# Attention maxima interleaved with halves of the scores, and turned before they are combined

## The chip, the cores and the metric

The kernel runs on one core of a Trainium2 chip. The metric is device time in microseconds (us) of one execution; lower is better. The core has TensorE (PE in the rows, with its weight loads as PEld), VectorE (DVE), ScalarE (ACT), GpSimd (POOL) and SyncE (SP), each with an instruction queue of its own, worked off in order. They synchronise by semaphores.

## The reference

A small two-layer model runs on x of shape (4, 1024, 128): causal attention, an MLP, an RWKV-like time and channel mix, an MLP, a second causal attention, two mixtures of experts and a single-head attention. The change touches the two causal attentions of 16 heads alone. What they compute, per head:

```python
scores = einsum('bqhd,bkhd->bhqk', q, k)      # layer 0: head width 8, plus one shared rotary term of width 32
scores = where(causal, -inf, scores / scale)  # layer 1: latent of width 32
w = softmax(scores, axis=-1)
attn = einsum('bhqk,bkhd->bqhd', w, v)
```

## The kernel before, in words

`attention` (L619) serves both layers: layer 0 with G=4 heads in a group and 4 groups for a batch, layer 1 with G=2 and 8 groups. One step is one group of one batch, so layer 0 has 16 steps and layer 1 has 32. Queries and keys are held as bf16 pieces (hi, mid, lo), stacked along the contraction dimension.

The softmax is written so that the row maximum is subtracted inside the score matmul. It therefore has to be known before a step begins. The work for it runs ahead of the steps, in *maximum units*: one unit is one bf16 matmul of a block of 128 queries against at most 512 keys into a PSUM bank of `mx` (L801; there are two such banks, used in turn), and one VectorE reduction of that bank (L931 where no mask is needed, L935 with the causal mask, followed by the read of its accumulator). TensorE may write a bank of `mx` only when VectorE has read it (`s_mxf`). A group has 12G units: 8G *wide* ones (query blocks 7, 6, 5 and 4, two parts each) and 4G *narrow* ones (query blocks 3, 2, 1 and 0, of 512, 384, 256 and 128 keys).

A step goes through eight key blocks kb. For each head j, `scores` (L820) computes the transposed scores of 128 keys against all queries that see them: queries 0 to 511 are one half (for kb < 4 only), queries 512 to 1023 the other. Each half takes two matmuls (L833, L835) and, where it holds the diagonal, a 128-column mask matmul (L838). Both halves go to one of two double banks of `score`, and ScalarE takes the exponential of both in one instruction (L910), up to 1024 elements wide. After the scores of block kb come the f32 matmuls of `values` for block kb-1 (L855); after block 7 come those of blocks 6 and 7.

TensorE's order is written out by hand (L880 to L893). Behind the scores of each head in kb 0 to 3 stand two wide units of the next group; behind those of kb 5, 6 and 7 stand one, two and one narrow units of the group after next. VectorE goes through the same units in the same order. Behind the scores of kb 4, `turn_max` (L806) turns the finished maxima into rows. Before it, `finish_max` (L941) makes them out of the two parts with four small VectorE instructions, as bf16 hi and lo; after it, `copy_turned` (L954) copies the two turned pieces out of PSUM, which frees both banks of `mx`. SyncE sends the rows through DRAM into an extra row of the second query operand (L745, L747), which the next step waits for (L877). Behind the last narrow unit, VectorE copies the finished output out of PSUM (L993), sets the next values (L972), and only then begins the wide units of the next step.

Of the kernel before, what the change touches and what calls it, by code (L numbers as in the profile page):

```python
# [19 lines left out]
P = 128  # L20
# [598 lines left out]
def attention(nc, k, tag, cf, qp, kp, qs, ks, vsrc, o_scr, l_scr, m_scr):  # L619
# [15 lines left out]
    NPC = 8 * 4  # L635
    with ExitStack() as st:  # L636
# [8 lines left out]
        mneg = c.sb("mneg", [P, G * QT])  # L645
        mpc = c.sb("mpc", [P, 2, G * QT], BF16)
        mrow = c.sb("mrow", [G * QT, 2, P], BF16)
        osb = c.sb("osb", [P, 2, T])
        masked = c.sb("masked", [P, 2, CH], BF16)
        score = c.ps("score", [P, 2, 2, CH])  # L650
        outp = c.ps("outp", [P, 2, CH])
        mx = c.ps("mx", [P, 2, CH])
# [11 lines left out]
        s_dpassed = c.sem("vector_passed")  # L664
# [125 lines left out]
        def _(pe):  # L790
            def max_units(b, g, qts, j, u):

                n = b * GN + g
                R = cf.rows[0]
                for qt in qts:
                    for part in range(2 if qt >= 4 else 1):
                        lo, hi = part * CH, min((qt + 1) * P, (part + 1) * CH)
                        bank = mx[:, u % 2, :]

                        pe.wait_ge(s_mxf, n * MU + u + 1)  # L800
                        pe.matmul(bank[:, 0:hi - lo], Q0[0:R, g % 4, j, qt * P:(qt + 1) * P],  # L801
                                  K0[0:R, g % 4, j % KG, lo:hi], start=True, stop=True).then_inc(s_mx, 1)
                        u += 1
                return u

            def turn_max(b, g, u):  # L806
                n = b * GN + g

                pe.wait_ge(s_mc, 4 * n + 4)
                for p in range(2):  # L810
                    pe.wait_ge(s_mxf, n * MU + u + 1)
                    pe.transpose(mx[0:G * QT, u % 2, 0:P // 2].bitcast(BF16), mpc[:, p, :], k.identb[:]).then_inc(s_mx, 1)
                    u += 1
# [6 lines left out]
            def scores(b, g, kb, j):  # L820

                n = b * GN + g
                u = kb * G + j

                pe.wait_ge(s_exp, n * U + u + 1)
                for half in range(2):
                    lo, hi = max(half * CH, kb * P), (half + 1) * CH
                    if lo >= hi:
                        continue
                    diag = lo == kb * P  # L830
                    bank = score[:, u % 2, half, lo - half * CH:CH]
                    R0, R1 = cf.rows
                    pe.matmul(bank, K0[0:R0, g % 4, j % KG, kb * P:(kb + 1) * P], Q0[0:R0, g % 4, j, lo:hi],  # L833
                              start=True, stop=False)
                    last = pe.matmul(bank, K1[0:R1, g % 2, j % KG, kb * P:(kb + 1) * P], Q1[0:R1, g % 2, j, lo:hi],  # L835
                                     start=False, stop=not diag)
                    if diag:
                        last = pe.matmul(bank[:, 0:P], k.identb[:], k.maskkq[:], start=False, stop=True)  # L838
                last.then_inc(s_st, 1)

            def values(b, g, kb):
# [3 lines left out]
                pe.wait_ge(s_exp, n * U + (kb + 1) * G + 2)  # L845
# [14 lines left out]
            def all_max_units(b, g, parts, u):  # L860
                for qts in parts.values():
                    for j in range(G):
                        u = max_units(b, g, qts, j, u)
                return u

            await_rows0(0, 0)
            all_max_units(0, 0, WIDE, all_max_units(0, 0, NARROW, 0))
            turn_max(0, 0, NARROW_U + WIDE_U)
# [3 lines left out]
            def step(b, g):  # L872
# [6 lines left out]
                u1, u2 = NARROW_U, 0  # L879
                for kb in range(QT):  # L880
                    if kb == 5 and two:
                        await_rows0(*two)
                    for j in range(G):
                        scores(b, g, kb, j)
                        if kb in WIDE and one:
                            u1 = max_units(*one, WIDE[kb], j, u1)
                        if kb in NARROW and two:
                            u2 = max_units(*two, NARROW[kb], j, u2)
                    if kb == 4 and one:
                        turn_max(*one, u1)  # L890
                    if kb > 0:
                        values(b, g, kb - 1)
                values(b, g, QT - 1)  # L893

            over_batches(pe, step)

        @block.scalar
        def _(act):
            act.sem_inc(s_exp, 2)

            def step(b, g):
                n = b * GN + g
                for kb in range(QT):

                    act.wait_ge(s_pv, n * 8 + kb - 1 + NPC)
                    for j in range(G):
                        u = kb * G + j
                        act.wait_ge(s_st, n * U + u + 1)
                        src = score[:, u % 2, :, :].rearrange("p h t -> p (h t)")[:, kb * P:T]
                        act.activation(probs[:, kb % 2, j, kb * P:T], src, ACT.Exp,  # L910
                                       scale=cf.scale).then_inc(s_exp, 1)

            over_batches(act, step)

        @block.vector
        def _(dve):
            dve.sem_inc(s_mxf, 2)
# [4 lines left out]
            def reduce_units(b, g, parts, u):  # L922
                n = b * GN + g
                for qts in parts.values():
                    for j in range(G):
                        for qt in qts:
                            for part in range(2 if qt >= 4 else 1):
                                w = min((qt + 1) * P, (part + 1) * CH) - part * CH
                                dve.wait_ge(s_mx, n * MU + u + 1)
                                if part * CH + w < (qt + 1) * P:  # L930
                                    dve.reduce_max(mpart[:, part, j, qt:qt + 1], mx[:, u % 2, 0:w],  # L931
                                                   AX).then_inc(s_mxf, 1)
                                else:
                                    dve.sem_inc(s_dpassed, 1)
                                    dve.tensor_tensor_reduce(  # L935
                                        masked[:, u % 2, 0:w], mx[:, u % 2, 0:w], k.maskw[:, CH - w:CH], 1.0, NEG, ALU.add,
                                        ALU.max, mpart[:, part, j, qt:qt + 1]).then_inc(s_mxf, 1)
                                u += 1
                return u

            def finish_max(b, g, u):  # L941
                n = b * GN + g

                dve.wait_ge(s_mxf, n * MU + u + 2)
# [1967 lines left out]
```

## Time and profile before

| | |
|---|---|
| time, median of 3 runs | 3158.78 us (3158.69 to 3168.52) |
| time of the profiled execution | 3168.43 us, of which 3166.7 us are its span |
| PE busy | 2361.7 us (75%) |
| DVE busy | 1743.7 us (55%) |
| ACT busy | 1241.0 us (39%) |
| POOL busy | 488.8 us (15%) |

One execution is profiled, and its time agrees with the slowest of the three runs. A busy share is taken over the whole span, most of which is not attention; the page gives it for 40 equal slices as well. In slices 4 to 10 and 20 to 28, which the two attentions fill, PE is busy nine tenths or more, and the granted TensorE clock is nine tenths or more of full speed. DVE stands there at five to eight tenths and ACT at three to five. Recorded matmuls overlap their neighbours (each has some 0.16 us of latency in its duration), so what a matmul costs is read from the distance of one start to the next.

### The profile page before, as it was taken

The numbers are of one execution on the slowest core, as the hardware profiler recorded it, in microseconds if no ns is written. First come the engines' busy times: TensorE is split into PE (matmuls) and PEld (weight loads), VectorE is DVE, ScalarE is ACT, GpSimd is POOL, SyncE is SP. The second block draws the span as 40 slices with busy tenths as digits, with TensorE's granted clock in tenths as the row PEclk, the third lists the DMA queues.
The fourth block names the chain that finished last, engine by engine and source line by source line (L and its number), as shares of the span: only waits on it lengthen the run. The fifth ranks groups of instructions, "written<-read, shape, count | busy, mean of one in ns | idle before, by whom it ended". The sixth has DMA issues, their size and how long they took to land. (4 is left out here: it accounts for less than half of the span.)

```text
span 3166.7 us, 46665 instructions
## 1 busy us (share of the span) xinstructions
PE 2361.7 (75%) x13512; PEld 1225.4 (39%) x13512; DVE 1743.7 (55%) x5508; ACT 1241.0 (39%) x1983; POOL 488.8 (15%) x524
## 2 busy tenths in 40 slices
PE   4559999999956328866999999999677292877382
PEld 1114344343334126532443434444254271554262
DVE  4656666666344886265665655666365324576223
ACT  2405455555534644553444444444222141343141
POOL 1400000000003000032000000000043463033554
PEclk9759999999977659877999999999888596988686
DMA  4272444443030000233122121121120152000144
GB/s 130 76 144 45 86 76 85 86 85 60 11 103 3 1 8 28 64 110 109 44 57 54 45 55 42 48 64 37 60 83 21 52 142 81 3 4 15 40 138 129
DMA packets 177903, 199.81 MB, mean 63 GB/s; under 512 B 36384, under 2 KB 117920, under 8 KB 177568
## 3 DMA queue, kind: packets, MB, share of 16 engines
q1 hardware_dynamic: 160000, 173.72, 22.1%
q0 software_dynamic: 9216, 19.02, 1.8%
q10 hardware_dynamic: 8448, 4.20, 0.4%
q8 instruction: 111, 1.82, 0.2%
q14 instruction: 128, 1.05, 0.1%
HBM read 127.09 MB, written 69.76 MB: 62 GB/s over the span
## 5 line engine op out<-in xcount | busy, mean ns | idle before, releaser
L910 ACT ACTIVATE at_probs<-at_score 128x1024 f32<-128x1024 f32 (+7 forms) x1024 | 655.2, 652 | 872.8 <-PE at_score L835 539.1
L935 DVE CUSTOM_DVE_ANT_0 at_masked<-at_mx,g_maskw 128x512 bf16<-128x512 f32 (+3 forms) x1024 | 483.4, 486 | 180.9 <-PE at_mx L801 177.6
L801 PE MATMUL at_mx<-at_K,at_Q 96*128 96x512 bf16 (+7 forms) x1536 | 467.0, 344 | 119.0 <-DVE at_mpart L935 40.9
L833 PE MATMUL at_score<-at_Q,at_K 96*128 96x512 bf16 (+7 forms) x1536 | 504.1, 332 | 28.9 <-issue 14.3
L835 PE MATMUL at_score<-at_Q,at_K 98*128 98x512 bf16 (+7 forms) x1536 | 507.2, 331 | 0.0
L931 DVE TENSOR_REDUCE at_mpart<-at_mx 128x1 f32<-128x512 f32 x512 | 353.8, 691 | 265.3 <-PE at_mx L801 245.1
L855 PE MATMUL at_outp<-at_probs,at_vop 128*32 128x512 f32 (+6 forms) x3072 | 445.2, 497 | 0.0
L801 PEld LDWEIGHTS at_mx<-at_K,at_Q 120*128 120x128 bf16 (+1 forms) x1536 | 148.4, 98 | 440.3 <-DVE at_mpart L935 198.6
L833 PEld LDWEIGHTS at_score<-at_Q,at_K 120*128 120x128 bf16 (+1 forms) x1536 | 149.8, 98 | 339.3 <-issue 183.1
L1025 POOL MEMSET n_spread<- 16x128 f32 (+1 forms) x2 | 0.7, 356 | 1541.0 <-POOLq L636 1541.0
L838 PE MATMUL at_score<-g_maskkq,g_identb 128*128 128x128 bf16 x1024 | 225.3, 220 | 0.0
L855 PEld LDWEIGHTS at_outp<-at_probs,at_vop 128*32 128x32 f32 (+1 forms) x3072 | 125.1, 122 | 108.1 <-issue 61.2
L835 PEld LDWEIGHTS at_score<-at_Q,at_K 122*128 122x128 bf16 (+1 forms) x1536 | 151.2, 98 | 22.2 <-issue 2.8
L1309 POOL TENSOR_TENSOR p_pieces<-p_rest,p_pieces 128x512 bf16<-128x512 f32 (+1 forms) x72 | 85.3, 1209 | 469.0 <-ACT p_pieces L1254 469.0
L838 PEld LDWEIGHTS at_score<-g_maskkq,g_identb 128*128 128x128 bf16 x1024 | 101.7, 99 | 52.1 <-issue 3.3
L993 DVE COPY at_osb<-at_outp 128x1024 f32<-128x1024 f32 x48 | 58.8, 1225 | 76.9 <-PE at_outp L855 76.9
L935 DVE DVE_READ_ACCUMULATOR2_ANT at_mpart<- 128x1 f32 x1024 | 85.6, 84 | 0.0
L2597 POOL DMA_INDIRECT back<-m1e_ye,m1e_target x80 | 76.8, 961 | 55.4 <-DVE m1e_ye L2588 32.6
L2597 POOL DMA_INDIRECT back<-m0e_ye,m0e_target x80 | 76.8, 960 | 55.1 <-DVE m0e_ye L2588 31.9
L1628 PE MATMUL wkv_out<-wkv_wo,wkv_y 128*128 128x128 f32 x64 | 15.0, 429 | 90.8 <-DVE b_zt L1607 54.2
L1928 POOL DMA_INDIRECT buf<-m1x_z,m1x_slot x64 | 66.7, 1042 | 78.7 <-DVE m1x_slot L2067 60.4
L1928 POOL DMA_INDIRECT buf<-m0x_z,m0x_slot x64 | 66.4, 1038 | 77.5 <-DVE m0x_slot L2067 59.3
(467 smaller groups left out, 3408.6 us busy)
## 6 DMA issues: line engine op xcount, KB each, us to landing
at_Q<-q SPq DMA_DIRECT2D x192, 128.0 KB, 3.0
at_Q<-qr SPq DMA_DIRECT2D x72, 256.0 KB, 5.9
at_K<-kr SPq DMA_DIRECT2D x72, 256.0 KB, 6.9
q<-p_pieces SPq DMA_DIRECT2D x40, 384.0 KB, 3.3
at_K<-k SPq DMA_DIRECT2D x168, 64.0 KB, 2.1
buf<-g_zeros SPq DMA_DIRECT2D x32, 325.0 KB, 5.0
o<-at_osb SPq DMA_DIRECT2D x64, 128.0 KB
n_oc<-o SPq DMA_DIRECT2D x8, 1024.0 KB, 5.0
```

The costliest lines, as they stand in the source:

```text
L801: pe.matmul(bank[:, 0:hi - lo], Q0[0:R, g % 4, j, qt * P:(qt + 1) * P], K0[0:R, g % 4, j % KG, lo:hi], start=True, stop=True).then_inc(s_m ...
L833: pe.matmul(bank, K0[0:R0, g % 4, j % KG, kb * P:(kb + 1) * P], Q0[0:R0, g % 4, j, lo:hi], start=True, stop=False)
L835: last = pe.matmul(bank, K1[0:R1, g % 2, j % KG, kb * P:(kb + 1) * P], Q1[0:R1, g % 2, j, lo:hi], start=False, stop=not diag)
L838: last = pe.matmul(bank[:, 0:P], k.identb[:], k.maskkq[:], start=False, stop=True)
L855: last = pe.matmul(outp[M * j:M * (j + 1), half, lo - half * CH:CH], vop[:, g % 2, kb, j % VG, :], probs[:, kb % 2, j, lo:hi], start=(kb = ...
L910: act.activation(probs[:, kb % 2, j, kb * P:T], src, ACT.Exp, scale=cf.scale).then_inc(s_exp, 1)
L931: dve.reduce_max(mpart[:, part, j, qt:qt + 1], mx[:, u % 2, 0:w], AX).then_inc(s_mxf, 1)
L935: dve.tensor_tensor_reduce(masked[:, u % 2, 0:w], mx[:, u % 2, 0:w], k.maskw[:, CH - w:CH], 1.0, NEG, ALU.add, ALU.max, mpart[:, part, j, ...
L993: dve.tensor_copy(osb[:, g % 2, :], outp[:].rearrange("p h t -> p (h t)")).then_inc(s_oev, 1)
L1309: pool.tensor_tensor(pcs[n][:, g, LO, :], rest[0:it.rows, n, :], pcs[n][:, g, MID, :], ALU.subtract).then_inc(s_lo, 1)
L1928: pool.indirect_dma_start(buf, bass.IndirectOffsetOnAxis(ap=slot[:, n, t:t + 1], axis=0), z[:, t, :], None).then_inc(s_out, 16)
L2597: pool.indirect_dma_start(back, bass.IndirectOffsetOnAxis(ap=target[:, e, t:t + 1], axis=0), ye[:, e % YR, t, :], None).then_inc(s_o[e % Y ...
```

## The change

- A unit of scores is now one half of one head (one bank out of four) instead of both halves (two banks out of four). ScalarE takes the exponential of each half by itself: 12G instructions in a step instead of 8G.
- In kb 0 to 3 one wide unit stands behind each half, instead of two behind both halves.
- The narrow units are spread: one behind the values of block 3, one behind each head in kb 5, 6 and 7 (block 5 thus begins on the second of them), and the last G-1 behind the values of block 7.
- The two parts of the maxima are turned by themselves, as f32, with no VectorE work before. VectorE then takes the larger of the two, negates it and splits it into hi and lo, all on the turned rows: four instructions of 128 columns, the last three of which read the banks of `mx`; both banks are freed at the end of the four.
- The unused half of `mpart` is filled once, in each attention, before the first turn.

```diff
-    U = QT * G
-    MU = 12 * G + 2
-    NARROW = {5: [3], 6: [2, 1], 7: [0]}
-    WIDE = {0: [7], 1: [6], 2: [5], 3: [4]}
+    SB, MB = 4, 2
+    U = 12 * G
+    MU = 12 * G + MB
+    NARROW = [(qt, 0, j) for qt in (3, 2, 1, 0) for j in range(G)]
+    WIDE = [(qt, part, j) for qt in (7, 6, 5, 4) for j in range(G) for part in range(2)]
...
-        score = c.ps("score", [P, 2, 2, CH])
+        score = c.ps("score", [P, SB, CH])
...
             def turn_max(b, g):
                 n = b * GN + g
-                pe.wait_ge(s_mc, 4 * n + 4)
-                for p in range(2):
-                    pe.wait_ge(s_mxf, n * MU + u + 1)
-                    pe.transpose(mx[0:G * QT, u % 2, 0:P // 2].bitcast(BF16), mpc[:, p, :], k.identb[:]).then_inc(s_mx, 1)
+                u = NARROW_U + WIDE_U
+                pe.wait_ge(s_mxf, n * MU + u + MB)
+                for part in range(2):
+                    pe.transpose(mx[0:G * QT, (u + part) % MB, 0:P], mpart[:, part, :, :].rearrange("p j q -> p (j q)"),
+                                 k.ident[:]).then_inc(s_mx, 1 + part * (MB - 2))
...
-            def scores(b, g, kb, j):
+            def scores(b, g, kb, j, half):
-                pe.wait_ge(s_exp, n * U + u + 1)
-                for half in range(2):
+                h = half_units(kb) + len(halves(kb)) * j + halves(kb).index(half)
+                pe.wait_ge(s_exp, n * U + h + 1)
+                bank = score[:, h % SB, lo - half * CH:CH]
...
                 for kb in range(QT):
-                    if kb == 5 and two:
+                    if kb == 4 and two:
                         await_rows0(*two)
                     for j in range(G):
-                        scores(b, g, kb, j)
-                        if kb in WIDE and one:
-                            u1 = max_units(*one, WIDE[kb], j, u1)
-                        if kb in NARROW and two:
-                            u2 = max_units(*two, NARROW[kb], j, u2)
+                        for half in halves(kb):
+                            scores(b, g, kb, j, half)
+                            if kb < 4:
+                                next_wide()
+                        if kb > 4:
+                            next_narrow()
                     if kb == 4 and one:
-                        turn_max(*one, u1)
+                        turn_max(*one)
                     if kb > 0:
                         values(b, g, kb - 1)
+                    if kb == 4:
+                        next_narrow()
                 values(b, g, QT - 1)
+                for _ in range(G - 1):
+                    next_narrow()
...
-                        src = score[:, u % 2, :, :].rearrange("p h t -> p (h t)")[:, kb * P:T]
-                        act.activation(probs[:, kb % 2, j, kb * P:T], src, ACT.Exp,
-                                       scale=cf.scale).then_inc(s_exp, 1)
+                        for half in halves(kb):
+                            lo, hi = max(half * CH, kb * P), (half + 1) * CH
+                            act.wait_ge(s_st, n * U + h + 1)
+                            act.activation(probs[:, kb % 2, j, lo:hi], score[:, h % SB, lo - half * CH:CH], ACT.Exp,
+                                           scale=cf.scale).then_inc(s_exp, 1)
...
+            dve.memset(mpart[:, 1, :, 0:4], NEG).then_inc(s_filled, 1)
...
-                dve.wait_ge(s_mxf, n * MU + u + 2)
-                dve.tensor_tensor(mpart[:, 0, :, 4:8], mpart[:, 0, :, 4:8], mpart[:, 1, :, 4:8], ALU.max).then_inc(s_mc, 1)
-                dve.tensor_scalar(mneg[:], m, -1.0, None, ALU.mult).then_inc(s_mc, 1)
-                dve.tensor_copy(mpc[:, 0, :], mneg[:]).then_inc(s_mc, 1)
-                dve.tensor_tensor(mpc[:, 1, :], mneg[:], mpc[:, 0, :], ALU.subtract).then_inc(s_mc, 1)
+                parts = [mx[0:G * QT, (u + part) % MB, 0:P] for part in range(2)]
+                larger = mx[0:G * QT, u % MB, P:2 * P]
+                dve.wait_ge(s_mx, n * MU + u + MB)
+                dve.tensor_copy(first[:], parts[0]).then_inc(s_mc, 1)
+                dve.tensor_tensor(larger, parts[1], first[:], ALU.max).then_inc(s_mc, 1)
+                dve.tensor_scalar(mrow[:, 0, :], larger, -1.0, None, ALU.mult).then_inc(s_mc, 1)
+                dve.scalar_tensor_tensor(mrow[:, 1, :], larger, -1.0, mrow[:, 0, :], ALU.mult,
+                                         ALU.subtract).then_inc(s_mrow, 2)
+                dve.wait_ge(s_mrow, 2 * n + 2)
+                dve.sem_inc(s_mxf, MB)
```

Each of the four instructions waits for the one before it (the waits on `s_mc` are left out above).

## Rows read from the trace of the kernel before

**Rows 1.** One line's answer, L993, the output copy that ends each step.
```profile
L993 DVE COPY at_osb<-at_outp x48: 1224/1225/1226, 266.5 to 2267.7; 128x1024 f32<-128x1024 f32 x48
```
**Rows 2.** Stretches of a layer-0 step: us; PE, PEld, DVE, ACT, POOL busy; PEclk; DMA share, GB/s.
```profile
514.52:525.95 11.43, 11.18 (x61) 4.94 (x57) 10.20 (x24) 7.26 (x8) 0.00 (x0) 1.00 0.53 122
527.80:538.75 10.95, 10.62 (x76) 4.69 (x72) 6.82 (x21) 5.80 (x8) 0.00 (x0) 1.00 0.91 176
540.18:542.63 2.45, 2.25 (x16) 0.89 (x13) 0.36 (x2) 1.48 (x3) 0.00 (x0) 1.00 0.52 87
542.63:546.58 3.95, 3.95 (x36) 1.86 (x34) 2.09 (x7) 2.30 (x6) 0.00 (x0) 1.00 0.12 27
547.58:554.06 6.48, 5.46 (x48) 2.81 (x44) 4.28 (x21) 2.33 (x7) 0.00 (x0) 1.00 0.01 3
514.52:554.76 40.24, 38.45 (x278) 16.61 (x274) 27.50 (x88) 20.61 (x32) 0.00 (x0) 1.00 0.51 104
```
**Rows 3.** The same for a layer-1 step.
```profile
1707.94:1713.79 5.85, 5.64 (x30) 2.45 (x28) 5.30 (x12) 3.39 (x4) 0.00 (x0) 1.00 0.33 90
1715.66:1721.93 6.27, 6.15 (x39) 2.69 (x37) 2.96 (x9) 2.79 (x4) 0.00 (x0) 1.00 0.07 23
1724.46:1727.21 2.75, 2.75 (x20) 1.17 (x19) 0.77 (x3) 1.31 (x4) 0.00 (x0) 1.00 0.01 3
1728.22:1731.57 3.35, 2.92 (x24) 1.50 (x22) 1.82 (x8) 0.95 (x3) 0.00 (x0) 1.00 0.00 0
1707.94:1732.38 24.44, 23.67 (x141) 9.90 (x139) 14.97 (x48) 10.28 (x16) 0.00 (x0) 1.00 0.16 45
```
**Rows 4.** Timeline, two score matmuls in succession: start us, us, what.
```profile
523.61 0.38 PE L833 MATMUL at_score<-at_Q,at_K 120*128 120x512 bf16 x1
523.83 0.38 PE L835 MATMUL at_score<-at_Q,at_K 122*128 122x512 bf16 x1
```
**Rows 5.** Timeline, kb 3: a wide pair, its reduction, the next pair.
```profile
534.87 0.43 PE L801 MATMUL at_mx<-at_K,at_Q 120*128 120x512 bf16 x2
535.28 0.69 DVE L931 TENSOR_REDUCE at_mpart<-at_mx 128x1 f32<-128x512 f32 x1 [1.78 <-PE at_mx L801]
...
536.03 0.39 PE L801 MATMUL at_mx<-at_K,at_Q 120*128 120x512 bf16 x1
```
**Rows 6.** Timeline, kb 5: a masked unit and the next one in its bank.
```profile
544.32 0.38 PE L801 MATMUL at_mx<-at_K,at_Q 120*128 120x512 bf16 x1
...
544.89 0.69 DVE L935 CUSTOM_DVE_ANT_0 at_masked<-at_mx,g_maskw 128x512 bf16<-128x512 f32 x1 [1.43 <-PE at_mx L801]
...
545.65 0.39 PE L801 MATMUL at_mx<-at_K,at_Q 120*128 120x512 bf16 x1
```
**Rows 7.** Groups by form, masked reductions of 128 elements: count, busy us, mean ns.
```profile
L935 DVE CUSTOM_DVE_ANT_0 at_masked<-at_mx,g_maskw 128x128 bf16<-128x128 f32 x256 | 72.8, 286 | 27.7 <-PE at_mx L801 27.1
```
**Rows 8.** Timeline, DVE at the start of the step.
```profile
514.75 1.22 DVE L993 COPY at_osb<-at_outp 128x1024 f32<-128x1024 f32 x1 [0.46 <-PE at_outp L855]
...
516.08 0.68 DVE L931 TENSOR_REDUCE at_mpart<-at_mx 128x1 f32<-128x512 f32 x1
```
**Rows 9.** Timeline, two bf16 turns, and eight f32 turns of another stage.
```profile
1724.46 0.28 PE L812 MATMUL at_mx<-g_identb,at_mpc 128*16 128x128 bf16 x2
...
2731.51 1.04 PE L2686 MATMUL sh_turn<-g_ident,sh_pr 128*128 128x128 f32 x8
```
**Rows 10.** Groups by form, small DVE instructions that read PSUM.
```profile
L958 DVE COPY at_mrow<-at_mx 32x128 bf16<-32x128 bf16 x32 | 6.8, 212 | 37.8 <-PE at_mx L812 35.4
L2784 DVE SCALAR_TENSOR_TENSOR g_xs<-sh_o,sh_ls,g_xs 128x128 f32<-128x128 f32 x8 | 2.8, 351 | 4.3 <-PE sh_o L2696 4.1
L2774 DVE COPY sh_prT<-sh_turn 128x128 f32<-128x128 f32 x8 | 2.3, 287 | 1.7 <-PE sh_turn L2686 1.7
```
**Rows 11.** Timeline, exponentials of 1024 elements, and two of 512 back to back.
```profile
515.66 1.03 ACT L910 ACTIVATE at_probs<-at_score 128x1024 f32<-128x1024 f32 x1 [2.01 <-PE at_score L835]
...
540.89 1.09 ACT L910 ACTIVATE at_probs<-at_score 128x512 f32<-128x512 f32 x2 [1.87 <-PE at_score L838]
```

More of the change, by code:

```diff
@@ L858, in values, with all_max_units @@
                 last.then_inc(s_pv, 1)
[L860 to L864, printed above, removed]
+            def all_max_units(b, g, units, u):
+                for i, unit in enumerate(units):
+                    max_unit(b, g, unit, u + i)
+            pe.wait_ge(s_filled, 1)
             await_rows0(0, 0)
-            all_max_units(0, 0, WIDE, all_max_units(0, 0, NARROW, 0))
-            turn_max(0, 0, NARROW_U + WIDE_U)
+            all_max_units(0, 0, NARROW, 0)
+            all_max_units(0, 0, WIDE, NARROW_U)
+            turn_max(0, 0)
             await_rows0(0, 1)
@@ L898, in _ @@
         def _(act):
-            act.sem_inc(s_exp, 2)
+            act.sem_inc(s_exp, SB)
             def step(b, g):
@@ L920, in _, with reduce_units @@
             dve.sem_inc(s_os[1], 16 * (G + 1))
-            def reduce_units(b, g, parts, u):
+            def reduce_units(b, g, units, u):
                 n = b * GN + g
[L924 to L939, printed above, removed]
@@ L954, in copy_turned @@
-            def copy_turned(b, g, u):
-                n = b * GN + g
-                for p in range(2):
-                    dve.wait_ge(s_mx, n * MU + u + 1)
-                    ins = dve.tensor_copy(mrow[:, p, :], mx[0:G * QT, u % 2, 0:P // 2].bitcast(BF16))
-                    ins.then_inc(s_mrow, 1)
-                    dve.wait_ge(s_mrow, 2 * n + p + 1)
-                    dve.sem_inc(s_mxf, 1)
-                    u += 1
+                for qt, part, j in units:
+                    w = min((qt + 1) * P, (part + 1) * CH) - part * CH
+                    dve.wait_ge(s_mx, n * MU + u + 1)
+                    if part * CH + w < (qt + 1) * P:
+                        dve.reduce_max(mpart[:, part, j, qt:qt + 1], mx[:, u % MB, 0:w], AX).then_inc(s_mxf, 1)
+                    else:
+                        dve.sem_inc(s_dpassed, 1)
+                        dve.tensor_tensor_reduce(
+                            masked[:, u % MB, 0:w], mx[:, u % MB, 0:w], k.maskw[:, CH - w:CH], 1.0, NEG, ALU.add,
+                            ALU.max, mpart[:, part, j, qt:qt + 1]).then_inc(s_mxf, 1)
+                    u += 1
@@ L964, in wide_maxima @@
             def wide_maxima(b, g):
-                u = reduce_units(b, g, WIDE, NARROW_U)
-                finish_max(b, g, u)
-                copy_turned(b, g, u)
+                reduce_units(b, g, WIDE, NARROW_U)
+                finish_max(b, g)
             def values(b, g):
```

82 lines of the change are left out of this document (42 added, 40 removed).

## The prediction

> **What bounds the kernel now.** I read the busy shares by slice first: in both attentions PE is the engine that is never far from full. Then the windows of one step each. The reader is to see in the whole-step rows that PE is busy 38.45 of 40.24 us in layer 0 and 23.67 of 24.44 us in layer 1, at the full clock (2.4 GHz), while DVE has 27.50 and 14.97 us and ACT 20.61 and 10.28 us [rows 2, 3]. The output copies show 48 steps, and their starts repeat at these distances [rows 1]. Recorded matmuls overlap, so "busy" hides bubbles. The price of a matmul is the distance of starts, 0.22 us for 512 columns (0.213 at 2.4 GHz) [rows 4], or 0.053 us for each 128 columns. Counted in columns, the narrow stretch kb 6 to 7 of layer 0 holds 4 x (640+640+384+128) = 7168 columns, 2.99 us, and one block of f32 values (0.78 us of the stretch). It takes 6.48 us [rows 2]. So 2.7 us of it are TensorE waiting, and those are the largest bubble of the step. I therefore price the change by walking TensorE's new order through the bank cycles of `mx`.
>
> **The bank cycle.** A reduction starts 0.41 us after the first matmul of its pair, and the bank is used again 1.16 us after that matmul (I take 1.17) [rows 5]. A masked unit of 512 takes 0.57 us to its start and 1.33 us in all [rows 6]. Each 128 fewer columns take off 0.053 us on PE and (0.687-0.286)/3 = 0.134 us on DVE (the 512 form is at 0.69) [rows 6, 7], so masked cycles of 384, 256 and 128 are 1.14, 0.95 and 0.77 us. With two banks, a unit can be placed every half cycle. DVE by itself is done with one after 0.61, 0.48, 0.34 and 0.30 us (its duration less the overlap of the next).
>
> **Kb 0 and 1.** TensorE needs per head 0.48 + 0.21 + 0.43 + 0.21 = 1.33 us in kb 0 and 1.17 us in kb 1. Before, the first reduction starts 1.56 us after the step (516.08 against 514.52) because DVE has the output copy to do [rows 8]. Now units stand behind the last values. In layer 0 there are three: the third waits for the bank of the first (0.77 us), so the step starts 0.82 us later, and the copy, behind three reductions, starts about 0.4 us later still relative to it. The first reduction is then at 1.98 us. The third wide unit wants its bank at 1.86 us and gets it at 1.98 + 0.75 = 2.73: a stall of 0.9 us, for which only 0.3 to 0.6 stood there before. Kb 0 ends at 6.24 us, kb 1 takes 4.85 (paced by 1.22 per head where DVE's masked unit pushes the reduction), together 11.1 against 11.43 [rows 2]: **-0.33**. Layer 1 has one unit in the tail, no wait behind it, but the copy starts 0.5 us later; the same walk ends at 6.12 against 5.85 [rows 3]: **+0.27**.
>
> **Kb 2 and 3.** The cycle of the unmasked bank, 1.17 us, is longer than TensorE's 1.01 and 0.85 per head, before and after. What is gained is the end: the last pair waited together for two banks, now its second part needs no wait. Kb 2: 0.27 + 3 x 1.17 + 0.75 = 4.53; kb 3: 0.16 + 3.51 + 0.69 = 4.36; with the values between (1.64) 10.53 against 10.95: **-0.42**. Layer 1: 2.19 + 1.66 + 2.02 = 5.87 against 6.27: **-0.40**.
>
> **Kb 4.** Before, a head's scores of 512 queries took a whole double bank, so the third head waited for ScalarE. Four half banks hold all four heads: 4 x 0.48 + 0.05 = 1.97 against 2.45 [rows 2]: **-0.48** in layer 0. With two heads nothing waits before or after: 0.
>
> **Turn to kb 5.** Two f32 turns cost 2 x 0.12 us (eight take 1.04 with 0.16 latency, so 0.11 each) against 2 x 0.06 [rows 9]: +0.1. DVE then has four dependent instructions of 128 columns. Row prices: copy 0.287, scalar_tensor_tensor 0.351; the two between I take at 0.29 and 0.28, by the copy; with four gaps of 0.035 us, 1.35 us [rows 10]. The new operands (32 or 16 partitions, one result in PSUM) are in no row. The low end is 4 x 0.212 + gaps = 1.0 us; the high end is 4 x 0.69 = 2.8 us, as if each cost a 512-wide reduction [rows 5, 10]. I take 1.35, because the width sets the time of such instructions [rows 7, 10]. Both banks stay held until 0.22 + 0.2 + 1.37 = about 1.84 us after the turn starts. TensorE reaches the first narrow unit after turn and values at 1.41: a wait of 0.43 us, with kb 5's scores queued behind. That work was free before, done by DVE ahead of the turn. With the moved unit (0.21) and one masked wait, the stretch is 4.62 against 3.95: **+0.67**; layer 1 3.31 against 2.75: **+0.56** [rows 2, 3]. The turned rows are complete about 0.8 us later than before; the next layer-1 step begins some 6 us after that (1732.38 against 1724.46 + 1.84) [rows 3], and I take their two small DMAs to fit into it.
>
> The Trainium skill (TensorE: Matmul & The Clock Gate, Part 4: PE-mode transpose) puts a 128x128 transpose at about 275 ns in a kernel. Row starts here put it at 0.06 us in bf16 and 0.12 us in f32, as its duration is mostly overlapped latency; by the page's figure taken as cost the two f32 turns would add 0.43 us instead of 0.1, and the total below would be 15 us less gain. The trace decides for the small figure.
>
> **Kb 6 and 7.** Before, two units per head met two banks: one whole cycle, 1.15 us, per head of kb 6 against 0.53 us of columns. Now one unit per head: kb 6 is 1.99 us (4 x 0.43 of columns and one wait of 0.27), the values stay 0.78, kb 7, with 256-wide units at 0.47 per head, 1.50. Sum 4.27 against 6.48: **-2.21**. Layer 1: 0.87 + 0.80 + 0.53 = 2.20 against 3.35: **-1.15** [rows 2, 3]. This is the gain.
>
> **Tail.** **+0.82** in layer 0, **+0.06** in layer 1, as above.
>
> **ScalarE.** 4G more instructions. Two of 512 take 1.09 us back to back, one of 1024 takes 1.03 [rows 11]: 0.06 us each, under 1.1 us in a step with 19 us idle. Hidden: TensorE needs 1.17 to 1.33 per head where ScalarE needs 1.09. If that cover goes, see the second rival.
>
> **Sum.** Maxima run ahead in 15 of 16 and 31 of 32 steps (wide), 14 and 30 (narrow). Layer 0: 15 x (-0.33-0.42-0.48) + 14 x (0.67-2.21+0.82) = -18.5 - 10.1 = -28.6. Layer 1: 31 x (0.27-0.40) + 30 x (0.56-1.15+0.06) = -4.0 - 15.9 = -19.9. Together -48.5 us. The prologues and the one-time fill are 0. Against the profiled 3168.43 us that is 3119.9. The median lies 9.65 us below the profiled execution, so the forecast is **3110 us**.
>
> **Rivals.** (1) *The chain on the turned rows holds both banks.* Place: the first narrow unit, kb 5 behind it. At the high end, 1.5 us more, in 44 steps: +66 us, 3176, slower than before. It decides from 48.5/44 = 1.1 us more, a chain of 2.5 us. For it: four dependent instructions, one writing PSUM, no row of the kind. Against: no 128-wide instruction in the rows is above 0.351 us [rows 10]. 8%.
> (2) *ScalarE paces kb 0 to 2.* If a half cost 0.12 us more than the back-to-back row shows, a head would need 1.45, 1.35 and 1.24 us against TensorE's 1.33, 1.22 and 1.17: 1.3 us a step in layer 0, 0.65 in layer 1, 15 x 1.3 + 31 x 0.65 = +40, 3150. Against it: 1.09 for two [rows 11]. The Trainium skill (ScalarE: Activation LUTs, Rules for kernel authors) budgets about 0.3 us per instruction beside 0.83 ns per element, which would be this rival; the 1.09 us speaks against it. 13%.
> (3) *The stalls I walked at the step start and in the tail don't add up*, since DVE catches up in kb 1: 0.9 us less in 46 steps, 3069. For it: DVE has 13 us free per step [rows 2]. Against: the copy stands in order ahead of the wide units [rows 8]. 7%.
>
> **How the numbers follow.** Forecast 69%, with +-0.4 us per step, +-20 us around 3110; the rest 3%. The range takes in this and most of rival 2, and the low end of the chain (0.35 x 44 = 15 us): 3088 to 3148. A change under 0.3% (9.5 us) can't be told from none. Faster: forecast, rival 3 and more than half of rival 2, 0.85; within 0.3%: 0.07; slower: rival 1, 0.08.
>
> **What would show it.** Right: steps of about 38.3 and 23.8 us; kb 6 of layer 0 near 2 us instead of 4.3; the four turned instructions 1.2 to 1.4 us from first start to last end; kb 4 at about 2.0. Wrong: an idle of over 1 us before the first narrow unit (rival 1), PE waiting for L910's successor in kb 0 (rival 2), or wide reductions that start within 1.6 us of the step (rival 3).

## The result, and the profile after

The changed kernel takes 3137.38 us (median of 4 runs, 3135.86 to 3142.82). The kernel before took 3160.11 us on the same chip. The ratio is 0.9926, 95% interval 0.9904 to 0.9947, so it is 23 us faster, where 48.5 us were forecast: a little under half. The direction came out as predicted, and 3137 lies inside the range of 3088 to 3148. The new waits stand where they were predicted, but one of the gains that were forecast, at the end of kb 3, isn't there, and part of the 23 us comes from places that the prediction had put at nothing.

The profiled execution after took 3142.82 us with a span of 3141.1 us, 25.6 us less than before. The page gives the busy times and the group of the exponentials:

```profile
PE 2329.6 (74%) x13512; PEld 1243.9 (40%) x13512; DVE 1759.8 (56%) x5414; ACT 1305.4 (42%) x2495; POOL 488.3 (16%) x524
L928 ACT ACTIVATE at_probs<-at_score 128x512 f32<-128x512 f32 (+3 forms) x1536 | 720.4, 491 | 780.9 <-PE at_score L838 613.3
```

ScalarE has 512 exponentials more and is busy 64.4 us longer, 0.126 us for each added one. TensorE's busy time fell by 32.1 us. The output copy is now L1001 (answers to [rows 1]):

```profile
L1001 DVE COPY at_osb<-at_outp x48: 1218/1224/1226, 264.7 to 2242.6; 128x1024 f32<-128x1024 f32 x48
```

The first copy starts 1.8 us earlier than before. From the first to the last one of layer 0, 18.2 us are gained; from there to the first one of layer 1, 2.4 us; within layer 1 only 2.7 us; and 0.5 us after it. Of the 18.2 us, 6.0 are in the last two steps of layer 0, for which the prediction had only 1.2. The steps of layer 0 repeat at 39.36 and 39.75 us (before: 40.25 and 40.70), those of layer 1 mostly at 24.30 to 24.32 (before: mostly 24.34 and 24.43). Forecast were 38.3 and 23.8.

The windows of one step of layer 0 stand in the order of [rows 2]: kb 0 and 1, kb 2 and 3, kb 4, turn to kb 5, kb 6 and 7, the tail, and the whole step. The step shown in [rows 2] is the fourth of its batch, this one is the third.

```profile
466.92:478.00 11.08, 10.66 (x56) 5.05 (x57) 10.66 (x26) 8.50 (x16) 0.00 (x0) 1.00 0.45 82
479.86:490.69 10.83, 10.46 (x77) 5.21 (x73) 7.71 (x22) 6.17 (x15) 0.00 (x0) 1.00 0.66 115
492.12:494.10 1.98, 1.98 (x16) 1.02 (x13) 0.00 (x0) 1.28 (x3) 0.00 (x0) 1.00 0.03 8
494.10:498.88 4.78, 4.54 (x37) 2.04 (x36) 3.46 (x11) 2.45 (x6) 0.00 (x0) 1.00 0.03 7
499.88:504.42 4.54, 4.22 (x44) 2.62 (x40) 2.76 (x13) 2.38 (x8) 0.00 (x0) 1.00 0.01 2
505.21:506.19 0.98, 0.49 (x8) 0.22 (x4) 0.55 (x4) 0.00 (x0) 0.00 (x0) 1.00 0.00 0
466.92:506.19 39.27, 37.44 (x275) 17.59 (x275) 27.92 (x86) 22.50 (x48) 0.00 (x0) 1.00 0.36 66
```

In a step of layer 1 (answers to [rows 3], where kb 4 was not shown either):

```profile
1684.40:1690.60 6.20, 5.53 (x31) 2.50 (x30) 5.76 (x14) 4.03 (x8) 0.00 (x0) 1.00 0.30 81
1692.47:1698.61 6.14, 6.02 (x39) 2.77 (x37) 3.58 (x10) 2.90 (x7) 0.00 (x0) 1.00 0.08 23
1701.05:1704.49 3.44, 3.21 (x21) 1.33 (x19) 2.14 (x7) 1.48 (x4) 0.00 (x0) 1.00 0.01 2
1705.50:1707.86 2.36, 2.36 (x23) 1.36 (x21) 1.00 (x4) 1.01 (x3) 0.00 (x0) 1.00 0.01 3
1684.40:1708.72 24.32, 23.30 (x140) 10.16 (x140) 15.28 (x46) 11.46 (x24) 0.00 (x0) 1.00 0.17 45
```

The reader is to see that the two stretches aimed at shrank (kb 4 from 2.45 to 1.98, kb 6 and 7 from 6.48 to 4.54), while the turn with kb 5 grew from 3.95 to 4.78 and a tail of 0.98 us is new. Kb 0 and 1 depend on the place of the step in its batch. Before the change they take, in the third step of the same batch:

```profile
473.91:485.25 11.34, 11.17 (x60) 4.96 (x57) 10.24 (x24) 7.25 (x8) 0.00 (x0) 1.00 0.49 88
```

So between third steps the gain is 0.26 us and not 0.35, and in the fourth step after the change (506.19 to 517.75) they take 11.56 us, 0.13 more than before. The mean over the layer's steps, without the two long ones behind a change of batch, is 11.23 against 11.39 us. The new waits are in the timeline of TensorE: behind the turn, in the tail, and at the start of the next step, which is the fourth of its batch.

```profile
533.85 0.38 PE L815 MATMUL at_mx<-g_ident,at_mpart 128*32 128x128 f32 x2
534.16 1.28 PE L855 MATMUL at_outp<-at_probs,at_vop 128*32 128x128 f32 x16
535.68 0.39 PE L806 MATMUL at_mx<-at_K,at_Q 120*128 120x512 bf16 x1 [0.24 <-DVEq L971]
```

```profile
505.21 0.29 PE L806 MATMUL at_mx<-at_K,at_Q 120*128 120x128 bf16 x2
505.99 0.23 PE L806 MATMUL at_mx<-at_K,at_Q 120*128 120x128 bf16 x1 [0.49 <-DVE at_mpart L950]
...
507.99 0.22 PE L838 MATMUL at_score<-g_maskkq,g_identb 128*128 128x128 bf16 x1
509.11 0.39 PE L806 MATMUL at_mx<-at_K,at_Q 120*128 120x512 bf16 x1 [0.90 <-DVE at_mpart L947]
```

VectorE's timeline shows what stands behind these waits: the chain on the turned rows (answers to [rows 9, 10]), and the copy ahead of the wide reductions (answers to [rows 8]).

```profile
534.26 0.28 DVE L962 COPY at_first<-at_mx 32x128 f32<-32x128 f32 x1 [3.28 <-PE at_mx L815]
534.58 0.29 DVE L964 TENSOR_TENSOR at_mx<-at_mx,at_first 32x128 f32<-32x128 f32 x1
534.90 0.28 DVE L966 TENSOR_SCALAR at_mrow<-at_mx 32x128 bf16<-32x128 f32 x1
535.29 0.28 DVE L968 SCALAR_TENSOR_TENSOR at_mrow<-at_mx,at_mrow 32x128 bf16<-32x128 f32 x1
```

```profile
507.02 1.22 DVE L1001 COPY at_osb<-at_outp 128x1024 f32<-128x1024 f32 x1 [0.32 <-issue]
...
508.37 0.68 DVE L947 TENSOR_REDUCE at_mpart<-at_mx 128x1 f32<-128x512 f32 x1
```

The chain takes 1.31 us, and its end frees both banks: the first narrow unit starts at 535.68, 1.83 us after the turn (predicted 1.84). In kb 0 the third wide unit stands 0.90 us idle here (predicted 0.9), and the first reduction starts 2.18 us after the step began (508.37 against 506.19; predicted 1.98). That is so in the fourth step of a batch alone (in three of the four batches). In the step of the windows the idle is less than half of it, and the first reduction starts 1.69 us after the step:

```profile
469.36 0.39 PE L806 MATMUL at_mx<-at_K,at_Q 120*128 120x512 bf16 x1 [0.41 <-DVE at_mpart L947]
```

In layer 1, but for the steps behind a change of batch, the idle is 0.54 to 0.68 us and the reduction starts at 1.82 to 1.95 us.

### The profile page after: what moved, and what is told of

The parts are those of the page before. It is cut to its first block and busy times, and to the rows that moved or that the text cites. A ratio compares the mean times of both kernels' runs of the same rounds, so it can differ in the third digit from the quotient of the medians.

```text
span 3141.1 us, 47721 instructions
## 1 busy us (share of the span) xinstructions
PE 2329.6 (74%) x13512; PEld 1243.9 (40%) x13512; DVE 1759.8 (56%) x5414; ACT 1305.4 (42%) x2495; POOL 488.3 (16%) x524
## 3 DMA queue, kind: packets, MB, share of 16 engines
q8 instruction: 111, 1.82, 0.3%
## 5 line engine op out<-in xcount | busy, mean ns | idle before, releaser
L928 ACT ACTIVATE at_probs<-at_score 128x512 f32<-128x512 f32 (+3 forms) x1536 | 720.4, 491 | 780.9 <-PE at_score L838 613.3
L806 PE MATMUL at_mx<-at_K,at_Q 96*128 96x512 bf16 (+7 forms) x1536 | 521.6, 343 | 132.5 <-DMA at_K<-k 36.2
L1001 DVE COPY at_osb<-at_outp 128x1024 f32<-128x1024 f32 x48 | 58.7, 1224 | 55.1 <-PE at_outp L855 54.1
L2605 POOL DMA_INDIRECT back<-m0e_ye,m0e_target x80 | 76.7, 958 | 55.3 <-DVE m0e_ye L2596 32.1
L962 DVE COPY at_first<-at_mx 16x128 f32<-16x128 f32 (+1 forms) x48 | 13.4, 279 | 121.1 <-PE at_mx L815 121.1
```

What stands on the lines that cost most here:

```text
L806: pe.matmul(mx[:, u % MB, 0:hi - lo], Q0[0:R, g % 4, j, qt * P:(qt + 1) * P], K0[0:R, g % 4, j % KG, lo:hi], start=True, stop=True).then_i ...
L928: act.activation(probs[:, kb % 2, j, lo:hi], score[:, h % SB, lo - half * CH:CH], ACT.Exp, scale=cf.scale).then_inc(s_exp, 1)
L1001: dve.tensor_copy(osb[:, g % 2, :], outp[:].rearrange("p h t -> p (h t)")).then_inc(s_oev, 1)
L2605: pool.indirect_dma_start(back, bass.IndirectOffsetOnAxis(ap=target[:, e, t:t + 1], axis=0), ye[:, e % YR, t, :], None).then_inc(s_o[e % Y ...
```

## Experiments

The kernels of the first four runs shared one chip and its runs of the kernel before (median 3163.05 us), the next four another (3164.20), the last two a third (3165.12). The changed kernel ran on the chip of the result (3160.11), so differences in us from it, and between runs of different chips, are good to some 5 us; where it matters the steps decide, most of which repeat to 0.05 us at the same place of a batch. Every one but the first starts from the changed kernel.

**One: halves of the scores alone**, put into the kernel before.

```diff
-        score = c.ps("score", [P, 2, 2, CH])
+        score = c.ps("score", [P, 4, CH])
...
-                        scores(b, g, kb, j)
+                        for half in halves(kb):
+                            scores(b, g, kb, j, half)
                         if kb in WIDE and one:
                             u1 = max_units(*one, WIDE[kb], j, u1)
```

> The kernel before with one part of the change alone: scores and exponentials in halves over four single banks; maxima, their places and their turn as before. Theory A (the gain of the change comes from both the half banks and the spread narrow units): kb 4 of layer 0 falls from 2.45 to about 2.0 us in 16 steps, the last steps of each layer, which have no maxima beside them, lose the 3.9 us that they lost with the whole change in layer 0; about -12 us in layer 0 and -4 us in layer 1, some 3144 us. Rival B (ScalarE's 512 added instructions cost something as soon as the maxima are not spread with them): no gain or a loss, 3160 us or more, and TensorE waiting for the exponentials in kb 0 and 1.

Measured: 3152.35 us, ratio 0.9973 (0.9962 to 0.9984). Windows of kb 0 and 1, of kb 4, and of the last step of layer 0, behind which no maxima are left to run ahead:

```profile
511.92:523.36 11.44, 11.19 (x61) 4.96 (x57) 10.20 (x24) 8.28 (x16) 0.00 (x0) 1.00 0.57 112
537.60:539.68 2.08, 2.08 (x17) 0.97 (x13) 0.35 (x2) 1.38 (x3) 0.00 (x0) 1.00 0.52 63
831.96:859.26 27.30, 27.23 (x224) 12.34 (x222) 1.23 (x1) 19.34 (x48) 0.00 (x0) 1.00 0.04 7
```

The same last step of the kernel before:

```profile
839.67:870.86 31.19, 28.76 (x224) 11.41 (x222) 1.23 (x1) 19.30 (x32) 0.00 (x0) 1.00 0.04 6
```

Rival B falls, but the gain is 8 to 11 us where theory A expected 16. Kb 4 gives 0.37 us of the 0.48. Kb 0 and 1 are unchanged (11.44 against 11.43) with 16 exponentials instead of 8 in them, so rival 2 of the prediction falls: ScalarE is busy 1.02 us more there and sets no pace. The trace of the changed kernel says it directly: in the steps of both attentions, none of TensorE's idle time is put down to ScalarE. The last step gains 3.89 us, which the prediction had not foreseen: without maxima between them, the scores met the two double banks again and again (twelve waits of TensorE for L910 in the last two steps of layer 0 before, none here), and four half banks end that. In layer 1 the steps stay as they were (24.34 and 24.44 us), and only the last one gains 0.5 us.

**Two: the old turn.** VectorE combines, negates and splits the columns before the turn, two bf16 transposes follow, and each copy frees one bank.

```diff
-                pe.wait_ge(s_mxf, n * MU + u + MB)
-                for part in range(2):
-                    pe.transpose(mx[0:G * QT, (u + part) % MB, 0:P], mpart[:, part, :, :].rearrange("p j q -> p (j q)"),
...
+                pe.wait_ge(s_mc, 4 * n + 4)
+                for p in range(2):
+                    pe.wait_ge(s_mxf, n * MU + u + 1)
+                    pe.transpose(mx[0:G * QT, u % MB, 0:P // 2].bitcast(BF16), mpc[:, p, :], k.identb[:]).then_inc(s_mx, 1)
```

> The changed kernel with the old turn: four small VectorE instructions on the columns ahead of it, two bf16 turns, two copies. Theory A (the four dependent instructions behind the turn hold both banks and TensorE waits for them at the first narrow unit): the stretch from turn to the end of kb 5 falls by 0.4 to 0.45 us, in 44 steps, so about 18 us less, 3119 us. Rival B (the wait is made good later in kb 5 and 6 anyway, or the small instructions ahead of the turn become a new wait): within 5 us of the changed kernel, 3132 to 3142 us.

Measured: 3121.49 us, ratio 0.9870 (0.9854 to 0.9887), 16 us better than the change. Turn to kb 5:

```profile
491.09:495.32 4.23, 4.23 (x38) 1.95 (x36) 2.76 (x9) 2.35 (x6) 0.00 (x0) 1.00 0.03 8
```

4.23 us against 4.78: the first narrow unit finds its bank free, as theory A has it. Turning first costs 0.46 to 0.8 us in a step of layer 0 (38.90 and 38.95 against 39.36 and 39.75) and 0.31 in layer 1 (23.99 to 24.01).

**Three: the narrow units where they were** (one, two and one behind the heads of blocks 5, 6 and 7, no tail).

```diff
-                        if kb > 4:
+                        for _ in range({5: 1, 6: 2, 7: 1}.get(kb, 0)):
                             next_narrow()
...
-                    if kb == 4:
-                        next_narrow()
-                for _ in range(G - 1):
-                    next_narrow()
```

> The changed kernel with the narrow units where they were: one, two and one behind each head of kb 5, 6 and 7, none behind the values of block 3, none in the tail. Theory A (the prediction's walk: kb 6 and 7 gain 1.9 us in layer 0 and 1.0 us in layer 1, tail and late copy give about 1.5 and 0.4 us of it back, and the wait behind the turn moves off the path): kb 6 and 7 long again, tail gone, kb 0 and 1 about 0.5 and 0.4 us shorter, turn to kb 5 about 0.6 us shorter; the sum near zero, 3130 to 3145 us. Rival B (spreading the narrow units is the gain of the change): 20 us slower, 3157 us or more.

Measured: 3143.75 us, ratio 0.9947 (0.9930 to 0.9963). Kb 0 and 1, and kb 6 and 7:

```profile
464.69:475.54 10.85, 10.66 (x60) 5.05 (x57) 10.43 (x24) 8.50 (x16) 0.00 (x0) 1.00 0.46 80
496.83:503.26 6.43, 5.32 (x48) 2.87 (x44) 4.46 (x21) 2.27 (x7) 0.00 (x0) 1.00 0.00 1
```

Theory A holds. Kb 6 and 7 lose 1.89 us, but kb 0 and 1 win back 0.23, turn to kb 5 0.59 (4.19) and the tail 0.98. The step is 39.37 us, as with the change, and the intervals of the two ratios overlap. So the gain the prediction called "the gain" is real in its stretch and paid back in three others.

**Four: wide units in pairs behind both halves.**

```diff
                         for half in halves(kb):
                             scores(b, g, kb, j, half)
-                            if kb < 4:
-                                next_wide()
+                        if kb < 4:
+                            next_wide()
+                            next_wide()
```

> The changed kernel with two wide units behind both halves of a head, as before, instead of one behind each half. Theory A (single units shorten the end of kb 0 to 3 by about 0.15 us each, and cost nothing else): 0.3 to 0.5 us a step slower, about 15 us, 3152 us. Rival B (the single units bring nothing in kb 0 and 1, because the first of them want their bank earlier while VectorE is still at the output copy): kb 0 and 1 the same or shorter, and the time within 5 us of 3137 us.

Measured: 3158.11 us, ratio 0.9982 (0.9968 to 0.9995), some 20 us worse than the change. Kb 0 and 1 (of the fourth step of a batch), and kb 2:

```profile
511.92:523.80 11.88, 11.33 (x56) 4.94 (x56) 10.49 (x26) 8.27 (x16) 0.00 (x0) 1.00 0.53 115
485.29:490.09 4.80, 4.80 (x32) 2.35 (x29) 3.22 (x10) 3.68 (x8) 0.00 (x0) 1.00 0.88 170
```

The steps are 39.97 and 40.37 us, and 24.48 to 24.50 in layer 1. What the single units buy in layer 0 is mostly in kb 0 and 1: 0.3 to 0.5 us (11.56 instead of 11.88 in this step, 11.08 instead of 11.57 in the third of the batch). In kb 2 it is 0.13 us, and in kb 3 nothing (4.52 in both). Rival B falls, and theory A has the total roughly but not the places.

**Five: no tail.** The last narrow units go behind earlier values.

```diff
-                    if kb == 4:
+                    if kb in ((4, 5, 6, 7) if G == 4 else (4, 5)):
                         next_narrow()
-                for _ in range(G - 1):
-                    next_narrow()
```

> The changed kernel with the units of the tail placed behind values instead: in layer 0 one narrow unit behind the values of blocks 3, 4, 5 and 6 each, in layer 1 behind those of blocks 3 and 4; nothing stands behind the last values. Theory A (tail and late output copy give back the gain of the spread narrow units): tail 0.98 us gone, the first wide reduction at 1.6 instead of 2.2 us after the step begins, kb 0 and 1 about 0.5 us shorter, the units behind values at 0.1 to 0.2 us of columns each; about 1.2 us a step in layer 0 and 0.35 us in layer 1, 27 us less than the changed kernel, 3110 us. Rival B (the start of a step is paced by VectorE's own work and banks, not by when the copy begins): only the tail's 0.98 us in layer 0 goes, 12 us, 3125 us.

Measured: 3129.91 us, ratio 0.9899 (0.9878 to 0.9920), some 8 us better than the change. Kb 6 and 7 with the unit ahead of them, then the last values with theirs:

```profile
500.56:505.76 5.20, 4.77 (x47) 2.75 (x43) 3.64 (x17) 2.50 (x8) 0.00 (x0) 1.00 0.01 2
505.76:506.85 1.09, 1.09 (x19) 0.41 (x18) 0.53 (x5) 0.15 (x1) 0.00 (x0) 1.00 0.07 15
```

The tail of 0.98 us is gone, but kb 6 and 7 take 5.20 us instead of 4.54. So most of the tail's price moves with its units: behind values they find the two banks no freer. The first reduction is at 1.48 to 1.57 us in most steps, as theory A expected, but kb 0 and 1 are only 0.22 us shorter and not 0.5, and the total lies above both theories. The step is 39.03 us instead of 39.36.

Experiments two and five together:

> The changed kernel without a tail (as in the run that has this alone) and with the old turn. If the two costs are separate places of the step, their gains add: the run without a tail less the 16 us that the old turn brought, 3094 us. If the wait behind the turn and the tail were one shortage of VectorE that moves from place to place, the two together bring little more than one of them, 3110 us.

Measured: 3114.59 us, ratio 0.9852 (0.9833 to 0.9872). The two add up: 16 and 8 us taken from the change give 3114. So do their steps. In layer 0 they are 38.57 and 38.69 us, 0.79 and 1.06 less than with the change, against 0.46 + 0.33 and 0.80 + 0.26; in layer 1 they are 23.83 and 23.93. The wait behind the turn and the tail are separate costs. What was expected at 3094 was too low because it took the run without a tail at 3110.

**Six: a third bank for the maxima**, taken from the scores.

```diff
-    SB, MB = 4, 2
+    SB, MB = 3, 3
```

> The changed kernel with three banks for the maxima and three for the scores, instead of two and four. Theory A (kb 0 to 3 are paced by the cycle of a bank of the maxima, 1.17 us for two units, and not by VectorE's own work): kb 2 about 4.1 instead of 4.7 us, kb 3 about 3.5 instead of 4.5 us, kb 0 and 1 some 0.6 us less, tail 0.6 us less, kb 4 about 0.2 us longer; 3 us a step in layer 0 and 1.1 us in layer 1, 3060 us. Rival B (VectorE's own work, 1.22 us for two units of 512, paces): 10 us less at most. Rival C (three score banks make TensorE wait for the exponentials all through): kb 0 and 1 longer, no gain.

Measured: 3052.58 us, ratio 0.9648 (0.9629 to 0.9667). Kb 2 and 3 with the values between:

```profile
463.04:472.58 9.54, 9.54 (x76) 4.94 (x72) 7.26 (x22) 6.17 (x15) 0.00 (x0) 1.00 0.78 135
```

9.54 us against 10.83, with TensorE busy in all of it. The step is 36.22 us, and 22.96 in layer 1. Rivals B and C fall. The bank cycle had set the pace wherever maximum units stand from kb 2 on, the tail included; kb 0 and 1 gain only 0.13 us (10.95 against 11.08) from the bank alone, and come to 10.36 only in the next experiment, without the tail and with the old turn.

**Seven: third bank, old turn and no tail together.**

> Three banks for the maxima and three for the scores, no tail, and the old turn: all that the runs so far point to. If the gains add: 3060 us less 16 for the turn, less 15 for the tail and the early copy (the tail's own wait is gone with three banks already), about 3030 us. If VectorE or ScalarE becomes the bound before that, 3045 us or more, with PE idle in kb 0 behind DVE (ahead of the third and fourth unit) or in kb 4 behind ACT.

Measured: 3023.04 us (runs from 3019.65 to 3028.15), ratio 0.9556 (0.9538 to 0.9574). The whole step, kb 3, and from kb 6 to the last values:

```profile
444.73:480.34 35.61, 35.61 (x275) 17.02 (x274) 27.10 (x90) 22.41 (x48) 0.00 (x0) 1.00 0.40 73
462.73:466.36 3.63, 3.63 (x33) 2.04 (x29) 3.03 (x10) 2.57 (x7) 0.00 (x0) 1.00 0.57 70
474.84:480.11 5.27, 5.27 (x63) 3.13 (x59) 3.98 (x21) 2.60 (x8) 0.00 (x0) 1.00 0.01 3
```

This is 114 us less than the changed kernel and some 140 less than the kernel before. TensorE's recorded busy time fills the step.

**Eight: the same three banks with the units in their old order** (edits of three and four on top of seven).

> Three banks for the maxima, three for the scores, the turn as before, and the maximum units where they stood before: two wide ones behind both halves of a head, narrow ones behind the heads of blocks 5, 6 and 7 (one, two, one), none behind the values. Against the last version (3023 us) only the order of the units is changed. Theory A: the interleaving worked only because two banks gave one unit per 1.17 us; a third bank gives two of three cycles back, so the old order costs little: 3023 to 3035 us. Theory B: a pair without scores between keeps its own stall (its second unit comes 0.22 us after the first, the next pair wants two banks at once), worth what it was worth with two banks, 0.6 us in 15 steps and 0.18 in 31, and the two narrow units of block 6 another 0.3 us in 44: 3050 us or more.

Measured: 3053.99 us, ratio 0.9641 (0.9625 to 0.9657). Kb 6 to the last values, and the whole step:

```profile
481.39:487.50 6.11, 5.64 (x64) 3.27 (x61) 4.58 (x24) 2.53 (x8) 0.00 (x0) 1.00 0.02 5
451.25:487.73 36.48, 36.02 (x276) 16.96 (x274) 27.04 (x89) 22.20 (x48) 0.00 (x0) 1.00 0.39 72
```

Theory B holds: some 30 us worse than seven (27 by the ratios). The step is 36.29 and 36.48 us against 35.43 and 35.61, in layer 1 22.91 and 23.09 against 22.39 and 22.57. From kb 6 to the last values it takes 6.11 us for twelve narrow units against 5.27 for eleven, and kb 3 takes 3.82 against 3.63. TensorE idles again in the first of these although there are three banks: two units in succession wait, one unit between scores does not. So the interleaving is still worth its time with a third bank. With two banks its two halves came to about as much (6 us in experiment three and 20 in four).

**Nine: seven with the tail.**

> The last version with the narrow units where the change put them: one behind the values of block 3, one behind each head in blocks 5 to 7, the last G-1 behind the values of block 7. Theory A: with three banks the tail's third unit waits for no bank, so the tail costs its columns alone (0.2 us) and DVE has slack in block 0: 3023 +- 9 us. Theory B: the output copy still starts later and the first reduction with it, 0.4 us in 14 steps and 0.2 in 30: 3035 us.

Measured: 3034.18 us, ratio 0.9579 (0.9563 to 0.9595). The tail itself:

```profile
479.25:479.63 0.38, 0.38 (x8) 0.21 (x4) 0.13 (x2) 0.00 (x0) 0.00 (x0) 1.00 0.09 22
```

It is 0.38 us where it was 0.98. In other steps it is 0.18 to 0.24. The steps are 35.78 and 22.67 us against 35.43 to 35.61 and 22.39 to 22.57, which is theory B by the steps; the intervals of the two whole-kernel ratios overlap.

## Why the prediction was half right

By its own steps, in us for one step (predicted, then measured, before against after, from the windows shown):

| | layer 0 | layer 1 |
|---|---|---|
| kb 0 and 1 | -0.33, -0.35 | +0.27, +0.35 |
| kb 2 and 3 | -0.42, -0.12 | -0.40, -0.13 |
| kb 4 | -0.48, -0.47 | 0, -0.09 |
| turn to kb 5 | +0.67, +0.83 | +0.56, +0.69 |
| kb 6 and 7 | -2.21, -1.94 | -1.15, -0.99 |
| values 6 and 7 | 0, 0 | 0, 0 |
| tail | +0.82, +0.98 | +0.06, +0.06 |
| step | -1.95, -1.06 | -0.66, -0.12 |

Two of the layer-0 figures need care. The window of the whole step in [rows 2] ends 0.09 us before the last values do, whose matmuls have the same recorded length of 0.86 us before and after. And kb 0 and 1 gain 0.16 us in the mean and not 0.35, so that their agreement with -0.33 is luck: kb 0 and kb 1 were walked at 6.24 and 4.85 us and took 6.05 and 5.03, and the two steps compared stand at different places of their batches. By the distance of output copies a step of layer 0 gains 0.89 to 0.95 us.

**Right.** Every sign, the place of each new wait, kb 4, the chain (1.31 us for 1.35), the moment when the banks come free (1.83 for 1.84), and rivals 1 and 3 dismissed by their own marks: the chain stayed far under 2.5 us, and the first reduction starts mostly 1.67 to 2.18 us into the step, not under 1.6 (it comes close to that mark in three steps of layer 0, at 1.55 and 1.60). The stall in kb 0 has its predicted size in three steps alone and is smaller in the others.

**The step that failed** is the walk of "Kb 2 and 3" and its like in "Kb 6 and 7", "Turn to kb 5" and "Tail": I set the new order, walked in pure column times, against a measured stretch of the old one. The measured stretch holds the small gaps, the walk does not. For kb 2 and 3 the term was nothing but this. By the prediction's own rules the old order takes as long as the new one: one head's scores ahead of the first pair, three cycles, the last pair. That is 0.70 + 3.51 + 0.32 = 4.53 us in kb 2 and 0.59 + 3.51 + 0.27 = 4.37 in kb 3, against 4.53 and 4.36 for the new order. "The last pair waited together for two banks" is not what the trace of before shows in kb 3. The pair ran through, and the values began 0.37 us after its start, where its columns need 0.27:

```profile
538.38 0.45 PE L801 MATMUL at_mx<-at_K,at_Q 120*128 120x512 bf16 x2
538.75 1.50 PE L855 MATMUL at_outp<-at_probs,at_vop 128*32 128x256 f32 x16
```

The timeline of kb 3 after shows the same gap:

```profile
486.17 0.23 PE L833 MATMUL at_score<-at_Q,at_K 120*128 120x128 bf16 x1
...
486.36 0.38 PE L806 MATMUL at_mx<-at_K,at_Q 120*128 120x512 bf16 x1
...
489.87 0.39 PE L806 MATMUL at_mx<-at_K,at_Q 120*128 120x512 bf16 x1
...
490.54 0.22 PE L806 MATMUL at_mx<-at_K,at_Q 120*128 120x128 bf16 x1
490.69 0.64 PE L855 MATMUL at_outp<-at_probs,at_vop 128*32 128x256 f32 x8
```

Three bank cycles from 486.36 to 489.87 are 3.51 us, exactly as walked. The start is 0.19 instead of 0.16, and from the last wide unit to the values it is 0.82 instead of 0.69, of which 0.15 alone lie between the last unit and the f32 values. The stretch is 4.52 where I had 4.36, and before it was 4.51: no gain at all. In kb 2 the mechanism is there, but it is worth 0.13 us in both layers (4.80 to 4.67, 2.45 to 2.32): its last pair before, at 532.05 us, is recorded with 0.62 us instead of 0.45, and the weight load of its second unit waits for L935. Experiment four says the same from the other side. Kb 2 and 3 were thus over-valued by 0.30 and 0.27 us a step, 13 us in all. The tail, the turn with kb 5 and kb 6 and 7 were short by 0.13 to 0.27 us each, except for the tail of layer 1. Together this makes some 0.9 us a step in layer 0 and 0.54 in layer 1. A few per cent of a stretch are little, but the net was the small difference of large terms, -2.2 against +0.7 and +0.8. In layer 1, where 0.66 was all that was left, the gaps took it: 17 of the 23 us missed are there (-19.9 predicted, -2.7 measured in the profiled executions).

**A second miss, in the kernel's favour.** I priced the halves at kb 4 alone. The last two steps of layer 0 gained 2.1 and 3.9 us (36.91 to 34.78, 31.19 to 27.30); the four half banks alone gave 1.7 and 3.9 in experiment one. The last two of layer 1 gained 0.7 more. Ahead of, between and behind the attentions another 4.8 us went, which no experiment explains; the profiled execution before was itself one of the slow ones of its runs, 8 us above the median, the one after 5. So of the 25.6 us between the profiled executions only some 15 come from the stretches that the prediction had priced at 48.5, and that the total came out near half of it is partly luck.

**Sizes.** The turn costs 0.31 us from its start to the values (I had 0.24 for two transposes). The Trainium skill (TensorE: Matmul & The Clock Gate, Part 4: PE-mode transpose) gives about 275 ns for one in a kernel, which by my estimate would be 0.55 for two in a row; the trace is nearer to the small figure, as taken. An added exponential costs ScalarE 0.126 us (I had 0.06), hidden all the same. The Trainium skill (ScalarE: Activation LUTs, Rules for kernel authors) budgets about 0.3 us per instruction, but for one whose bias is a [128,1] pointer operand. Our exponentials are given no bias, so the prediction's second rival used a figure for another form; 0.126 us is what the added ones cost here.

**Left open.** One in three steps within a batch of layer 0 is 0.4 us longer than the others, before and after (40.70 against 40.25, 39.75 against 39.36). Before, it shows in kb 7 (1.77 us against 1.42). After, it shows at the output copy, whose 0.32 us of idle name no releaser, and it is nearly gone with the old turn (38.90 and 38.95 in experiment two); why is not shown. And two of the three crossings to the next batch cost 4.5 to 7 us in every kernel, the third costs under 0.4 us. That was not tried.

## What to carry to other kernels

When a new order is walked, walk the old one by the same rules and take the difference, or give every block its measured gap; a model compared with a measurement carries its whole bias into the answer. Where two buffers cycle between engines slower than the work between them, first count what a third buffer gives: here it was worth 85 us, the whole change 23. Taken one at a time, by medians, the parts of the change come to about 10 us for the halves, 20 for the single wide units, 6 for the spread narrow ones (within the noise) and 16 lost by the new turn, which adds up to about the 23 measured. An instruction chain that holds such a buffer belongs ahead of the point where the buffer is taken.

## What the runs showed of the hardware

- The bank cycle, one 512-column matmul, its reduction on VectorE and the release, is 1.17 us with two units in flight, in kb 2 and in kb 3 alike, though the scores between differ. With a third bank kb 3 of layer 0 takes 3.63 us instead of 4.52, close to its columns (3.4 to 3.5 us, estimated from 0.213 to 0.22 us for 512 columns).
- An f32 block of values starts 0.15 us after a 128-column unit whose columns need 0.05 us.
- Where no maxima are between, three half banks for the scores are not as good as four: the last step of layer 0 takes 28.44 us in experiments six to nine (copies at 767.03 and 795.47 in seven) against 27.30. In layer 1 the last step takes 18.62 us against 18.43. These are the only stretches looked at in which the third bank's loan costs more than it gives.
- VectorE instructions of 128 columns on 32 rows of PSUM take 0.28 to 0.29 us, and follow each other at 0.32 to 0.39 us when each needs the one before.
